# Latent attention: four banks for the output products of a head, and another order of queries, outputs and scores within a pair

## The reference, cut to what matters

```python
q_hk = (hidden_q @ Wq.T).reshape(Bv, Sv, H, K)
q_big = jnp.einsum('bshk,hkq->bshq', q_hk, w_kc_q)
q_big = _apply_rope(q_big, sin_q[None, :, None, :], cos_q[None, :, None, :])
kv_r = _apply_rope(kv_c, sin_k[None], cos_k[None])
q_r = jnp.einsum('bshq,hqr->bhsr', q_big, W_qr)
k_r = jnp.einsum('bld,hdr->bhlr', kv_r, W_kr)
scores = jnp.einsum('bhsr,bhlr->bhsl', q_r, k_r)
attn = jax.nn.softmax(scores, axis=-1)
ctx_c = jnp.einsum('bhsl,bld->bhsd', attn, kv_r)
ctx_lat = jnp.einsum('bhsd,hkd->bhsk', ctx_c, w_kc_kv)
ctx = ctx_lat.transpose(0, 2, 1, 3).reshape(Bv, Sv, H * K)
return ctx @ Wo.T
...
x = x + jnp.tanh(g_xattn[3]) * _L3_xattn_ref(_layernorm(x, axis=-1), ctx_512, ...)
```

## Time and profile before

| | us |
|---|---|
| median of 3 runs | 3797.08 (3795.95 to 3798.74) |
| profiled execution, whole | 3797.58 |
| its span in the trace | 3795.8 |
| TensorE matmuls busy in the span | 3552.7 (94%) |
| VectorE busy | 2174.4 (57%) |
| ScalarE busy | 1406.2 (37%) |

### The profile page before, as it was taken

The page is one execution under the profiler, slowest core; times in us unless marked ns, Lnnn a source line. Parts: engine busy times, 40 slices in busy tenths (PEclk is TensorE's granted clock), DMA queues, the critical chain, the costliest instruction groups (busy, mean ns, idle before and its releaser), DMA issues.

```text
span 3795.8 us, 38099 instructions
## 1 busy us (share of the span) xinstructions
PE 3552.7 (94%) x12973; PEld 1916.1 (50%) x12974; DVE 2174.4 (57%) x3831; ACT 1406.2 (37%) x2908; POOL 627.8 (17%) x588
## 2 busy tenths in 40 slices
PE   5999999996889999599959999999999999999999
PEld 1444444442445444366524444444444445888888
DVE  7656666235678777311137665656565665655554
ACT  7524343111357667222223444444343443111111
POOL 5100000000132331211111100000000002544543
PEclk7999999998989999799979999999999999999999
DMA  7321312210422323555542100010101002111220
GB/s 235 133 74 67 128 63 71 111 45 26 95 64 57 90 63 86 182 163 160 162 155 71 48 27 36 25 38 25 38 25 38 25 26 89 67 67 45 78 78 23
DMA packets 81846, 294.03 MB, mean 77 GB/s; under 512 B 17928, under 2 KB 18824, under 8 KB 66832
## 3 DMA queue, kind: packets, MB, share of 16 engines
q1 hardware_dynamic: 74304, 269.32, 21.8%
q0 software_dynamic: 7376, 22.57, 1.9%
HBM read 248.31 MB, written 38.81 MB: 76 GB/s over the span
## 4 chain that ended last, share of the span: by engine, by line
PE 85%; DVE 9%; POOL 2%; DMA 2%; ACT 2%; issue 1%; SPq 0%; DVEq 0%; ACTq 0%; POOLq 0%
PE BM L2316 6%; PE BM L2376 6%; PE BM L444 5%; PE BR L444 5%; PE BR L2387 4%; PE BM L2751 3%; PE BS L2751 3%; PE BR L2751 3%; PE BS L460 3%; PE BT L460 3%; PE BT L2368 3%; PE BT L1589 3%; PE BR L2021 3%; PE BM L2329 3%; PE BM L2010 3%; PE BR L2010 2%
## 5 line engine op out<-in xcount | busy, mean ns | idle before, releaser
L2447 ACT COPY AR<-BM 128x512 f32<-128x512 f32 x320 | 187.5, 586 | 409.6 <-PE BM L2329 122.1
L2556 DVE SCALAR_TENSOR_TENSOR X<-BR,AR,X 128x512 f32<-128x512 f32 x256 | 189.0, 749 | 208.5 <-PE BR L2387 199.9
L228 POOL TENSOR_TENSOR RSTD<-VAR,HALF 128x4 f32<-128x4 f32 x32 | 34.6, 1081 | 1451.9 <-DVE VAR L2572 925.5
L2387 PE MATMUL BR<-AR 128*128 128x512 f32 x512 | 253.7, 618 | 12.7 <-DVE X L2556 11.3
L2376 PE MATMUL BM<-AR 128*128 128x512 f32 x512 | 246.4, 593 | 0.0
L444 PE MATMUL BM<-XT,AR 128*128 128x512 f32 x512 | 230.6, 593 | 0.9 <-ACT AR L598 0.9
L2316 PE MATMUL BM<-XT,AR 128*128 128x512 f32 x512 | 229.9, 602 | 0.7 <-ACT XT L241 0.7
L444 PE MATMUL BR<-XT,AR 128*128 128x512 f32 x512 | 230.2, 592 | 0.0
L1681 ACT ACTIVATE PT<-BS 128x512 f32<-128x512 f32 x340 | 191.9, 596 | 73.4 <-PE BS L1579 68.2
L605 ACT ACTIVATE AR<-AR 128x512 f32<-128x512 f32 x256 | 182.5, 714 | 83.3 <-DVE AR L733 79.7
L2543 DVE TENSOR_REDUCE AR<-BS 128x2 f32<-128x1024 f32 x64 | 78.5, 1227 | 215.9 <-PE BS L2356 215.9
(11 more groups left out here) (447 smaller groups left out, 6914.4 us busy)
## 6 DMA issues: line engine op xcount, KB each, us to landing
AR<-l_wq_dram SPq DMA_DIRECT2D x32, 1152.0 KB, 5.1
AR<-l_w_dram SPq DMA_DIRECT2D x36, 1024.0 KB, 4.9
AR<-l_w_dram SPq DMA_DIRECT2D x64, 512.0 KB, 3.3
AR<-l_w_dram SPq DMA_DIRECT2D x42, 768.0 KB, 4.8
AR<-w2h SPq DMA_DIRECT2D x16, 1024.0 KB, 4.8
QS<-qx SPq DMA_DIRECT2D x32, 512.0 KB, 9.5
AR<-l_w_dram SPq DMA_DIRECT2D x8, 1408.0 KB, 8.4
made<-AR SPq DMA_DIRECT2D x40, 256.0 KB, 4.8
```

Source lines behind the costliest of these rows:

```text
L2387: nc.tensor.matmul(BR[:, L3[job] % 2, :], CC3[h][:, st * P:(st + 1) * P], W3[:, p % 8 * 2 + h, :], start=True, stop=True)\
L2447: nc.scalar.copy(to, BM[:, L3[job] % 2, :]).then_inc(m_free, 1)
L2556: nc.vector.scalar_tensor_tensor(out=xb, in0=BR[:, L3[job] % 2, :], scalar=RS3[:, p % 2, h, st:st + 1], in1=xb, op0=ALU.mult, op1=ALU.add) ...
```

## The change

The output products get four banks in each call of `outputs`. A new function `out_bank` says which: `b2` of head h has `BR` bank h for good; the products of token tiles 2 and 3 have the two banks of `BR`; those of token tiles 0 and 1 have the two banks of `BT` for head 0 and the two of `BS` for head 1. For `outputs(30, 1)`, the group that stands in the last pair, the two halves are exchanged. `l3_earlier` finds for each job in `BR` the one that had the bank before. `out_home` issues the waits: for `BR` until that earlier job has been read, for `BT` in the pairs that turn a normalised tile until ScalarE has copied the last of it, for `BS` until the exp of scores 0 of the pair that runs has read the bank.

The scores wait for the adds in turn: scores 1 (`BT`) for the second add of `outputs(p-1, 0)`, scores 2 (`BS`) for the second add of `outputs(p-1, 1)`, in the last pair for the fourth.

The order changes on three engines. TensorE: after scores 1 come `head_queries(p+1, 0)` and `outputs(p-1, 1)`, and `head_queries(p+1, 1)` comes after scores 3. VectorE: `add_outputs(p-1, 1)` comes between the maxima 1 and 2. ScalarE: the copy of head 0's queries stays behind the exps of scores 1, that of head 1's comes behind those of scores 3. The arithmetic, the loads and the table `l3_table` are as they were.

```diff
+        def out_bank(job):
+            if job[0] == "b2":
+                return BR, job[2]
+            p, h, st = job[1:]
+            tile, j = divmod(st, 2)
+            if (p, h) == (NP3 - 2, 1):
+                tile = 1 - tile
+            return (BR if tile else (BT, BS)[h]), j
+
+        def l3_earlier():
+            earlier, last = {}, {}
+            for job in sorted((j for j in L3 if j[0] in ("b2", "out")), key=lambda j: L3[j]):
+                tile, j = out_bank(job)
+                if tile is BR:
+                    earlier[job], last[j] = last.get(j), job
+            return earlier
+        EARLIER3 = l3_earlier()
...
+            def out_home(job):
+                tile, j = out_bank(job)
+                if tile is BR and EARLIER3[job]:
+                    pe.wait_ge(o_free, L3[EARLIER3[job]] + 3)
+                if tile is BT and j == 0 and job[1] % 8 == 6:
+                    pe.wait_ge(t_free, L3["norm", job[1] // 8, KT - 1] + 3)
+                if tile is BS and job[1] < NP3 - 1:
+                    pe.wait_ge(exped[j], ST * (job[1] + 1) + 1)
+                return tile[:, j, :]
+
             def big_query(p, h, i):
...
-                    job = ("b2", p, h)
-                    pe.wait_ge(o_free, L3[job] + 1)
-                    nc.tensor.matmul(BR[:, L3[job] % 2, :], WS[:, p % 2, at + 2 * P:at + 3 * P], QHK[h], start=True, stop=True).then_inc(o_full, 1)
+                    nc.tensor.matmul(out_home(("b2", p, h)), WS[:, p % 2, at + 2 * P:at + 3 * P], QHK[h], start=True, stop=True).then_inc(o_full, 1)
...
                 if st == 1 and p:
-                    pe.wait_ge(t_free, (L3["norm", p // 8, KT - 1] if p % 8 == 7 else L3["turn", p - 1, 1, ST - 1]) + 3)
+                    pe.wait_ge(o_free, L3["out", p - 1, 0, 1] + 3)
+                if st == 2 and p:
+                    pe.wait_ge(o_free, L3["out", p - 1, 1, 1 if p + 1 < NP3 else ST - 1] + 3)
...
                 for st in range(ST):
-                    job = ("out", p, h, st)
-                    pe.wait_ge(o_free, L3[job] + 1)
-                    nc.tensor.matmul(BR[:, L3[job] % 2, :], CC3[h][:, st * P:(st + 1) * P], W3[:, p % 8 * 2 + h, :], start=True, stop=True)\
+                    nc.tensor.matmul(out_home(("out", p, h, st)), CC3[h][:, st * P:(st + 1) * P], W3[:, p % 8 * 2 + h, :], start=True, stop=True)\
                       .then_inc(o_full, 1)
...
                 scores(p, 1)
                 if more and p:
                     head_queries(p + 1, 0)
-                    head_queries(p + 1, 1)
-                if not more:
+                if p:
                     outputs(p - 1, 1)
                 scores(p, 2)
                 scores(p, 3)
                 if more and p:
-                    outputs(p - 1, 1)
+                    head_queries(p + 1, 1)
...
                         exp(p, st, h)
-                    if more and p and st == 1:
-                        for h in range(2):
-                            take(("q", p + 1, h), QHK[h])
+                    if more and p and st % 2 == 1:
+                        take(("q", p + 1, st // 2), QHK[st // 2])
...
                     maximum(p, st)
-                if p + 1 == NP3:
+                if p:
                     add_outputs(p - 1, 1)
                 for st in range(2, ST):
                     maximum(p, st)
-                if p and p + 1 < NP3:
-                    add_outputs(p - 1, 1)
```

More of the change, by code:

```diff
@@ L2528, in rotate @@
                 v.wait_ge(o_full, L3[job] + 1)
-                bank = BR[:, L3[job] % 2, :]
+                tile, j = out_bank(job)
+                bank = tile[:, j, :]
                 tt(rq[:, 2, :], bank, ROPE[:, 4, :], ALU.mult)
@@ L2555, in add_outputs @@
                     xb = X[:, p // 8 * ST + st, :]
-                    nc.vector.scalar_tensor_tensor(out=xb, in0=BR[:, L3[job] % 2, :], scalar=RS3[:, p % 2, h, st:st + 1], in1=xb,
+                    tile, j = out_bank(job)
+                    nc.vector.scalar_tensor_tensor(out=xb, in0=tile[:, j, :], scalar=RS3[:, p % 2, h, st:st + 1], in1=xb,
                                                    op0=ALU.mult, op1=ALU.add).then_inc(o_free, 1)
```

## The result

| | us |
|---|---|
| median before | 3797.91 (3795.95 to 3799.02) |
| median after | 3762.09 (3757.76 to 3764.61) |
| ratio after to before | 0.9905, 95% interval 0.9888 to 0.9922 |
| profiled execution after, whole | 3764.46 |
| its span | 3762.6 |

What follows compares the result with a forecast made beforehand. TensorE was taken to set the attention's pace, priced by its weight loads. Gains of 9.9 + 27.9 + 0.96 = 38.8 us from 3797.58 left 3758.8, forecast as 3758.5 us, range 3754 to 3775.

Steps and rivals of the forecast that it cites:

- the formula: A TensorE segment of n passes between two shape changes takes 0.54 + (n - 3) x 0.4285 + 0.95 us.
- Four banks: In outputs(p, 0), no product waits for its own group's adds: 3.63 us a segment, 31 x 0.32 = 9.9 us gained.
- The new order: Outputs(p-1, 1) moved between head 0's queries and scores 2: gain 0.93 us a pair, 30 times, 27.9 us.
- The last groups: Outputs(31, 0) and (31, 1) at the attention's end: 6.86 us in place of 7.82, gain 0.96.
- Pair 31: Last pair, where scores 2 wait for the fourth add: counted at nothing, may gain 0.7 us or lose about as much.
- (a): Scores 1 (bank BT) wait for the second add of outputs(p-1, 0); claimed cover 1.7 us.
- Y: Time of the first load of the query segment after scores 0 and 1.
- (d): Product big_query(p+1, 0, 2) waits for ScalarE's copy of head 1's queries; claimed cover 0.5 us, the thinnest.
- (b): First output product in BS waits until exp of scores 0, head 0, has read the bank; claimed cover 1.7 us.
- the second rival: Queries-to-outputs and queries-to-big_query joins cost a break each: 60 x 0.52 = 31 us, time 3790; chance 0.05.
- the first rival: One thin cover fails, head 1's query copy or an add late, breaking TensorE's stream: 15.6 us, 3774; chance 0.10.
- The slower rival: VectorE becomes the bound at the maxima, its chain holding the adds: at 3 us late, 20 us lost, 3817; chance 0.03.

Runs made afterwards that it cites:

- The second execution: The changed kernel profiled and timed once more, unaltered, against the kernel before: median 3761.6 us, ratio 0.9903, attention stretch 1161.6 us.

## Why the prediction was right, point by point

**What bounds the kernel.** Right. The pair followed from the count of weight loads and the breaks; every segment came out within 0.01 us of the formula (3.63, 7.06, 5.69).

**Four banks.** Right: 31 segments of 3.63; 10.0 us, where 9.9 had been put.

**The new order.** Right: 30 times 0.92 to 0.93. Of these 0.67 come with the order alone and 0.25 need the four banks, which the prediction took for granted in this term. The joins of one shape cost nothing, as the row of context and outputs had said; that breaks belong to the shape was shown by moving scores 1.

**The last groups.** Right for the two last ones (6.87 against 6.86). Pair 31, counted at nothing, lost some 0.2: its outputs and the scores behind them took 8.99 before and 9.23 after (3141.91 to 3151.14), since the wait for the fourth add stands there.

**The waits and their covers.** Right that all four hold; one size was misread. In (a) scores 1 load first 1.38 ahead of Y, at 2839.93; the Y - 0.96 of the prediction is their second pair of loads. The second add has ended at 2838.53, so the cover is 1.4 and not 1.7. (d) had 0.50, which three copies more used up. (b) is the one that the order pays for: without the queries in front it costs more than the whole change brings. The sign "no load at their line charged to an add" was too strict: 25 are, without a loss.

**The sum.** 38.8 us for the attention against 38.6 measured at the same granted clock; the difference is pair 31. The second execution shows 37.1, 1.5 of it lost to the clock in the last transposes, a term that the sum did not have. The sum also took the start of the attention as fixed at 2003.1, and it varies by 7 us between executions. In the first profiled execution, 6.0 us over the forecast (3764.46), 5.5 are this start. The second, at 3758.79, is within 0.3 of the forecast partly by luck: it started 1.7 early and lost 1.5 to the clock. The median came out 3.6 over the forecast, in the range; of the executions behind it only the first of the four has a trace. The prediction allowed 1.6 us for the scatter of the runs shown, which span 2.8; the after kernel's four span 6.9.

**The rivals.** None came true; their prices were mis-sized. I priced a break at 0.52 us (0.95 - 0.43) and left out the 0.32 that the two close loads behind it give back, though the segment formula had both. Two more shape changes cost 0.40 a pair, so the second rival would have been 60 x 0.20 = 12 us, a time of 3771 and not 3790; and three copies too many cost 0.30 a pair where the first rival had 0.52. The slower rival named VectorE's chain; the place that does make this order slower than before when its cover goes is the bank wait for the exps.

**The rule on draining.** The Trainium skill, TensorEngine Tiling (Array Packing), Key Properties, says that a change of the tiling mode drains TensorE. The traces agree: the idle 0.76 came with each of the two changes that were added. The price here is 0.20 us net, for fp32 products of 512 columns.

## What to carry to other kernels

Count a dense engine's stream in steps of its weight loads, with a net price for each break, and the effect of a reordering can be added up before it is tried. For a result bank that another engine empties, ask how long it is held (some 2 us here) against how often a product comes (0.86); two banks were too few here, and a second pair may be borrowed from a stage that rests then. The borrowed bank brings a wait of its own: put independent work of the same shape in front of it, and measure the cover.

## What the runs showed of the hardware that I had not expected

A change between 128-row and 64-row operands shows 0.52 us of extra idle time in front of the next weight load, yet costs 0.20, since the first two loads behind it come 0.11 us apart. And the time of identical code ahead of the attention differed by up to 7.2 us between profiled executions, with a granted clock of 0.66 to 0.81 over the same 30 us in three of them; and in six of the nine the clock fell again in the attention's last transposes, behind an idle of 3.5 us, for 0.7 to 1.5 us. So a few microseconds of a 3.8 ms kernel are better read from the stretch that was changed than from the whole, and two such stretches compared only after a look at the granted clock in both.
